# Softmax sums of two attention stages: from ones-matmuls on TensorE to column halving on GpSimd

## What is computed

```python
def _L1_xattn_ref(query, key, value, ...):      # causal; h = 16, hd = 8
    score = jnp.einsum('bqhd,bkhd->bhqk', q, k) / np.sqrt(hd)
    score = jnp.where(causal, score, -jnp.inf)
    probs = jax.nn.softmax(score, axis=-1)
    out = jnp.einsum('bhqk,bkhd->bqhd', probs, v).reshape(b, tq, d)
    return out @ Wo.T + bo
def _L2_xattn_ref(q, kv, Wq, Wkv, Wc):          # keys and values of one head's width, shared by 16 heads
    logits = jnp.einsum('bhld,bmd->bhlm', qh, mk) * scale
    attn = jax.nn.softmax(logits, axis=-1)
    out = jnp.einsum('bhlm,bmd->bhld', attn, mv)
```

## Time and profile before

| what | value |
|---|---|
| median of 3 runs | 3389.18 us (3385.43 to 3396.54) |
| profiled execution, its own time | 3393.09 us |
| span of the profiled execution | 3391.2 us |
| busy: PE / PEld / DVE / ACT / POOL | 79% / 54% / 65% / 36% / 13% of the span |
| layer 1 attention | about 410 to 735 us |
| layer 2 attention | about 1750 to 2135 us |

### The profile page before, as it was taken

The page is one execution under the profiler, slowest core; times in us unless marked ns, Lnnn a source line. Parts: engine busy times, 40 slices in busy tenths (PEclk is TensorE's granted clock), DMA queues, the critical chain, the costliest instruction groups (busy, mean ns, idle before and its releaser), DMA issues. The chain is left out here.

```text
span 3391.2 us, 66864 instructions
## 1 busy us (share of the span) xinstructions
PE 2683.7 (79%) x24521; PEld 1816.6 (54%) x24556; DVE 2218.8 (65%) x5515; ACT 1215.5 (36%) x1872; POOL 441.9 (13%) x749
## 2 busy tenths in 40 slices
PE   4867599958999999999978998797905658883456
PEld 4634356645666565666636666575704546662126
DVE  6889689963455555545437889772035558887668
ACT  3658688840000000000027776453301114442330
POOL 0022200000000000000000000241170004441003
PEclk9978699989999999999979999898957779997569
DMA  2010000012221212112100000101312210000001
GB/s 87 28 57 1 10 18 13 15 50 100 72 79 51 100 50 90 60 57 93 50 14 14 14 12 2 35 28 54 96 50 65 62 30 1 0 0 7 0 3 46
DMA packets 88410, 137.01 MB, mean 40 GB/s; under 512 B 42949, under 2 KB 54597, under 8 KB 87242
## 3 DMA queue, kind: packets, MB, share of 16 engines
q1 hardware_dynamic: 80746, 114.75, 10.5%
q0 software_dynamic: 7520, 20.34, 2.0%
HBM read 117.75 MB, written 17.30 MB: 40 GB/s over the span
## 5 line engine op out<-in xcount | busy, mean ns | idle before, releaser
L1435 PE MATMUL banks<-l1f_xe,l1f_w 128*128 128x512 f32 x1024 | 486.5, 598 | 10.4 <-DVE l1f_xe L1634 10.4
L1634 DVE TENSOR_TENSOR l1f_xe<-l1f_hT,l1f_rwb 128x512 f32<-128x512 f32 x256 | 173.5, 693 | 299.4 <-PE banks L1437 277.2
L1437 PEld LDWEIGHTS banks<-l1f_w,l1f_xe 128*128 128x128 f32 x2048 | 269.5, 192 | 122.9 <-issue 122.9
L1640 DVE TENSOR_TENSOR l1f_ae<-l1f_aoT,l1f_rwb 128x512 f32<-128x512 f32 x256 | 172.8, 691 | 160.2 <-PE banks L1465 155.8
L1437 PE MATMUL banks<-l1f_w,l1f_xe 128*128 128x128 f32 x2048 | 270.0, 275 | 0.0
L1435 PEld LDWEIGHTS banks<-l1f_xe,l1f_w 128*128 128x128 f32 x1024 | 177.3, 192 | 140.9 <-issue 126.9
L1465 PE MATMUL banks<-l1f_ae,l1f_w 128*128 128x512 f32 x512 | 225.2, 599 | 1.4 <-DVE l1f_ae L1640 1.4
L1465 PEld LDWEIGHTS banks<-l1f_ae,l1f_w 128*128 128x128 f32 x512 | 97.4, 193 | 117.9 <-issue 115.7
L223 PE MATMUL banks<-consts,l3p_h 128*128 128x128 f32 x64 | 17.8, 435 | 166.1 <-DVE l3p_h L140 166.1
L214 POOL COPY x<-xn 128x512 f32 (+1 forms) x16 | 9.8, 610 | 972.0 <-DVE xn L1664 972.0
L223 PEld LDWEIGHTS banks<-consts,l3p_h 128*128 128x128 f32 x64 | 11.5, 217 | 169.3 <-issue 132.2
(11 more groups left out here) (490 smaller groups left out, 6346.4 us busy)
## 6 DMA issues: line engine op xcount, KB each, us to landing
l1f_rwb<-l1f_shares SPq DMA_DIRECT2D x128, 512.0 KB, 4.3
l3p_ctx<-in_ctxT SPq DMA_DIRECT2D x32, 256.0 KB, 3.9
l0a_ctxT<-in_ctxT SPq DMA_DIRECT2D x16, 256.0 KB, 2.6
l2f_sent<-l0f_zero SPq DMA_DIRECT2D x4, 1024.0 KB, 7.0
l1a_ctxT<-in_ctxT SPq DMA_DIRECT2D x16, 256.0 KB, 2.6
l2c_ctxT<-in_ctxT SPq DMA_DIRECT2D x16, 256.0 KB, 2.6
l2e_rows<-l2f_sent SPq DMA_DIRECT2D x16, 256.0 KB, 2.8
l2f_answers<-l2e_y POOLq DMA_DIRECT2D x16, 256.0 KB, 2.7
```

Source lines behind the costliest of these rows:

```text
L1435: pe.matmul(bank, w[:, n, e, :], xe[:, e % NB, :], start=(e == 0), stop=(e == E - 1))
L1437: last = pe.matmul(v_bank[:, D * j:D * j + D], xe[:, e % NB, P * j:P * j + P], w[:, 2, e, :], start=(e == 0 and j == 0), stop=(e == E - 1) ...
L1634: dve.tensor_tensor(xe[:, e % NB, :], hT[:, m, :], rwb[:, m, e, :], ALU.mult).then_inc(s.xe_ready, 1)
L1640: dve.tensor_tensor(ae[:, e % NB, :], aoT[:, m, :], rwb[:, m, e, :], ALU.mult).then_inc(s.ae_ready, 1)
```

## The change

In both stages the sums no longer come from TensorE. A new part `total` on POOL adds the two halves of each head's 64 columns of `prob` (after the exponential): 64 to 32, 32 to 16, 16 to 8, three `tensor_tensor` adds of 128 x 512, 128 x 256 and 128 x 128 results, all in SBUF. `invert` on DVE sums the last 8 columns and takes the reciprocal of 16 numbers a token. `widen` on POOL copies each of the 16 numbers 8 times (128 x 128). `weigh` on PE transposes that one tile into PSUM in place of the eight ones-matmuls, and `normalise` on DVE copies it out of PSUM, where it took the reciprocal, before the same multiplication. `centre` has a further wait: for the first halving of two tiles before. In POOL's lists the new parts come between the old ones: layer 1 add_bias(n-1), widen(n-5), total(n-4), copy_mv(n-8); layer 2 keep_q(n-10), widen(n-15), total(n-14), copy_mv(n-19). On DVE `invert` stands behind `centre` and ahead of `normalise`.

```diff
     def weigh(self, pe, t, r):
+        pe.wait_ge(s.rec_ready, t + 1)
+        wait(pe, s.o_ready, t)
+        pe.transpose(self.rec_psum, self.rec[:, r % 2].rearrange("p h e -> p (h e)"), self.k.ident[:, :])
         pe.wait_ge(s.pT_ready, t + 1)
         pe.wait_ge(s.v_ready, t - j + TG)
-        wait(pe, s.o_ready, t)
-        for a in range(4):
-            for e in range(2):
-                pe.matmul(self.sum_psum[32 * a:32 * a + 32, :], self.k.pairsum[:, 32 * e:32 * e + 32], self.pT[:, r % 2, 2 * a + e, :],
-                          start=(e == 0), stop=(e == 1), skip_group_check=True)
...
         wait(dve, s.pT_psum, t - 1)
+        wait(dve, s.tree_chain, 2 * t - 3)
         dve.tensor_tensor(self.prob[:, r % 2], self.scores, self.top[:, :].unsqueeze(2).to_broadcast([P, H, S]),
                           ALU.subtract).then_inc(s.centred, 1)
+    def total(self, pool, t, r):
+        prob = self.prob[:, r % 2]
+        pool.wait_ge(s.exp_ready, t + 1)
+        settle(pool, self.k)
+        pool.tensor_tensor(self.half[:, :, :], prob[:, :, 0:S // 2], prob[:, :, S // 2:S], ALU.add).then_inc(s.tree_chain, 1)
+        pool.wait_ge(s.tree_chain, 2 * t + 1)
+        settle(pool, self.k)
+        pool.tensor_tensor(self.quarter[:, :, :], self.half[:, :, 0:S // 4], self.half[:, :, S // 4:S // 2], ALU.add).then_inc(s.tree_chain, 1)
+        pool.wait_ge(s.tree_chain, 2 * t + 2)
+        wait(pool, s.summed, t - 1)
+        settle(pool, self.k)
+        pool.tensor_tensor(self.eighth[:, r % 2], self.quarter[:, :, 0:S // 8], self.quarter[:, :, S // 8:S // 4], ALU.add)\
+            .then_inc(s.sum_ready, 1)
+    def invert(self, dve, t, r):
+        dve.wait_ge(s.sum_ready, t + 1)
+        settle(dve, self.k)
+        dve.tensor_reduce(self.sums[:, :], self.eighth[:, r % 2], AX_X, ALU.add).then_inc(s.summed, 1)
+        dve.wait_ge(s.summed, t + 1)
+        wait(dve, s.rec_ready, t)
+        dve.reciprocal(self.inverse[:, :], self.sums[:, :]).then_inc(s.inverted, 1)
+    def widen(self, pool, t, r):
+        pool.wait_ge(s.inverted, t + 1)
+        wait(pool, s.o_psum, t - 1)
+        settle(pool, self.k)
+        pool.tensor_copy(self.rec[:, r % 2], self.inverse[:, :].unsqueeze(2).to_broadcast([P, H, HD])).then_inc(s.rec_ready, 1)
     def normalise(self, dve, t, r):
         dve.wait_ge(s.o_psum, t + 1)
-        dve.reciprocal(self.rec[:, :], self.sum_psum).then_inc(s.rec_ready, 1)
-        dve.wait_ge(s.rec_ready, t + 1)
+        dve.tensor_copy(self.recT[:, :], self.rec_psum).then_inc(s.rec_copied, 1)
+        dve.wait_ge(s.rec_copied, t + 1)
         wait(dve, s.y_psum, t - 1)
-        dve.tensor_tensor(self.oT[:, r % 2], self.oT_psum, self.rec[:, :], ALU.mult).then_inc(s.o_ready, 1)
+        dve.tensor_tensor(self.oT[:, r % 2], self.oT_psum, self.recT[:, :], ALU.mult).then_inc(s.o_ready, 1)
```

More of the change, by code:

```diff
@@ L1004 @@
 CORE_SEMS = ("weights x_read biased xn_ready stats_chain stats_ready mv_copied q_ready k_ready v_ready score_psum max_ready "
-             "centred exp_ready pT_psum pT_ready o_psum rec_ready o_ready y_psum ")
+             "centred exp_ready tree_chain sum_ready summed inverted pT_psum pT_ready o_psum rec_ready rec_copied o_ready y_psum ")
 RING = 2 * TG
@@ L1023, in __init__ @@
         self.pT = sb("pT", [P, 2, 8, P])
-        self.rec = sb("rec", [P, P])
+        self.half = sb("half", [P, H, S // 2])
+        self.quarter = sb("quarter", [P, H, S // 4])
+        self.eighth = sb("eighth", [P, 2, H, S // 8])
+        self.sums = sb("sums", [P, H])
+        self.inverse = sb("inverse", [P, H])
+        self.rec = sb("rec", [P, 2, H, HD])
+        self.recT = sb("recT", [P, P])
         self.oT = sb("oT", [P, 2, P])
@@ L1029, in __init__ @@
         self.pT_banks = (ps[2], ps[3])
-        self.oT_psum, self.sum_psum = ps[4][:, 0:P], ps[4][:, P:2 * P]
+        self.oT_psum, self.rec_psum = ps[4][:, 0:P], ps[4][:, P:2 * P]
         self.y_psum = ps[5].rearrange("p (t c) -> p t c", c=D)
@@ L1107, in centre @@
         wait(dve, s.pT_psum, t - 1)
+        wait(dve, s.tree_chain, 2 * t - 3)
         dve.tensor_tensor(self.prob[:, r % 2], self.scores, self.top[:, :].unsqueeze(2).to_broadcast([P, H, S]),
                           ALU.subtract).then_inc(s.centred, 1)
+    def total(self, pool, t, r):
+        s = self.s
+        prob = self.prob[:, r % 2]
[11 more added lines that the diff above has]
+    def invert(self, dve, t, r):
+        s = self.s
+        dve.wait_ge(s.sum_ready, t + 1)
[5 more added lines that the diff above has]
+    def widen(self, pool, t, r):
+        s = self.s
+        pool.wait_ge(s.inverted, t + 1)
+        wait(pool, s.o_psum, t - 1)
+        settle(pool, self.k)
+        pool.tensor_copy(self.rec[:, r % 2], self.inverse[:, :].unsqueeze(2).to_broadcast([P, H, HD])).then_inc(s.rec_ready, 1)
     def normalise(self, dve, t, r):
@@ L1209, in _ @@
             pool.wait_ge(s.row_ready, 1)
-            pipeline(pool, k.NT, [(8, lambda t, r: core.copy_mv(pool, t, r)), (1, lambda t, r: core.add_bias(pool, t, r))],
+            pipeline(pool, k.NT, [(1, lambda t, r: core.add_bias(pool, t, r)), (5, lambda t, r: core.widen(pool, t, r)),
+                                  (4, lambda t, r: core.total(pool, t, r)),
+                                  (8, lambda t, r: core.copy_mv(pool, t, r))],
                      unroll=RING, behind=8)
@@ L1302, in feed @@
                     last.then_inc(s.x_read, TG)
-            pipeline(dve, k.NT, [(4, lambda t, r: core.centre(dve, t, r)), (6, lambda t, r: core.normalise(dve, t, r)),
+            pipeline(dve, k.NT, [(4, lambda t, r: core.centre(dve, t, r)), (5, lambda t, r: core.invert(dve, t, r)),
+                                 (6, lambda t, r: core.normalise(dve, t, r)),
                                  (7, lambda t, r: core.new_x(dve, t, r)), (0, feed)], unroll=RING, behind=8)
@@ L1743, in keep_q @@
                 pool.tensor_copy(core.qT[:, u, :], q[:, u, :]).then_inc(s.q_ready, TG)
-            pipeline(pool, k.NT, [(18, lambda t, r: core.copy_mv(pool, t, r)), (10, at_group(keep_q))], unroll=RING, behind=8)
+            pipeline(pool, k.NT, [(10, at_group(keep_q)), (15, lambda t, r: core.widen(pool, t, r)),
+                                  (14, lambda t, r: core.total(pool, t, r)),
+                                  (19, lambda t, r: core.copy_mv(pool, t, r))], unroll=RING, behind=8)
         @block.tensor
@@ L1888, in spread_v @@
                 last.then_inc(s.v_ready, TG)
-            pipeline(dve, k.NT, [(14, lambda t, r: core.centre(dve, t, r)), (16, lambda t, r: core.normalise(dve, t, r)),
+            pipeline(dve, k.NT, [(14, lambda t, r: core.centre(dve, t, r)), (15, lambda t, r: core.invert(dve, t, r)), (16, lambda t, r: core.normalise(dve, t, r)),
                                  (17, lambda t, r: core.add_x(dve, t, r)), (6, at_group(choose)), (8, at_group(store_v)),
```

## The result

The changed kernel takes 3431.78 us (median of 4 runs, 3422.11 to 3436.09) against 3390.76 for the kernel before beside it: a ratio of 1.0117, 95% interval [1.0088, 1.0145]. The interval lies above 1, so it is slower by more than the noise of the runs. The profiled execution took 3434.38 us with a span of 3432.8, 41.6 more than before.

The account below looks back on a forecast made before the run. It took DVE to limit two of four steps in layer 1, and PE two steps and DVE the `choose` step in layer 2. Layer 1 +25 us and layer 2 +5 us on 3389.2 gave 3419, range 3388 to 3452.

Parts of the forecast that it names:

- L1300 waits for POOL: Layer 1 layer norm on DVE: its SBUF instructions are held up by POOL's additions, 1.0 us a group.
- `choose` blocked: Layer 2, DVE: L1866 and the two comparisons L1873 wait for POOL's halvings, 1.0 us a group.
- `invert` waits 0.8 a group: Layer 1, DVE: POOL's sums come late for `invert`, by 0.3 and 0.5 us in two of four steps.
- step 2: Layer 1 step (tile modulo 4) with residual sum and statistics, limited by DVE; `invert` forecast 0.3 us late.
- step 0: Layer 1 step (tile modulo 4) with the layer norm, limited by DVE; `invert` forecast 0.5 us late.
- The earlier wait in `centre`: DVE's further wait for POOL's halving was to cost nothing, as it concerns work over 1 us back.
- I count no change of it: Granted clock, 0.98 in both stages before: taken to stay at the upper level, no time counted.
- The savings: Less work on DVE and PE: 0.25 us a group in layer 1, 2 x 0.29 plus 0.12 in layer 2.
- POOL as the bound: Rival: POOL's chain a tile takes over some 4.7 us and limits the group; +58 us, 3447; chance 0.13.
- nothing is blocked: Rival: sums late, but DVE slips through beside POOL; no change, 3391 us; chance 0.11.
- The adds are done in time: Rival: addition chain under 3.0 us, blocking under 0.2 a group, savings kept; -11 us, 3378; chance 0.08.
- The point on the reciprocal: Small SBUF reciprocal on DVE beside POOL's `add_bias`: up to 1.0 us a group if blocked; nothing counted.

Follow-up runs that it names:

- e1: Kernel before plus POOL's three additions, read by nobody, and the further wait in `centre`; sums still from PE: 3443.41 us, ratio 1.0171.
- e5: Changed kernel with layer norm ahead of `invert`, `add_bias` behind `total`, and every fourth tile's layer 2 halvings after the one-hot matrix: ratio 1.0019.
- e4: Changed kernel without the further wait in `centre`: ratio 1.0106 to the kernel before.
- e10: Changed kernel with the further wait in `centre` on another semaphore, `sum_ready` at t - 1 instead of `tree_chain` at 2 t - 3: ratio 1.0105.
- e6: Changed kernel with layer norm, `add_bias` and layer 2 halvings moved out of DVE's way, and without the further wait in `centre`: ratio 1.0005.
- e3: Changed kernel with eight more PE transposes a group, ahead of the h transposes (layer 1) and one-hot transposes (layer 2): ratio 1.0077.
- e2: Changed kernel with one 128 x 128 add for the three halvings (sums incomplete) and the further wait on `sum_ready`: ratio 0.9953.

## Why the prediction was right, and where it was not

The forecast of 3419 us, slower, with 3388 to 3452, was right in sign and held the time; it was 13 us short. Its main mechanism, POOL's long additions keeping DVE's instructions waiting, is shown. That the sum for layer 1 came so near is luck: too much for `invert` stands against two costs that were left out.

- **L1300 waits for POOL: right.** Forecast 1.0 us a group; measured 4 x (0.598 - 0.345) = 1.01. e1 and e5 show it as the cause: the stretch is there with additions that nobody reads, and gone when they are moved.
- **`choose` blocked: right.** Forecast 1.0; measured (1.096 - 0.425) + 2 x (0.550 - 0.419) = 0.93.
- **`invert` waits 0.8 a group: mis-sized.** In step 2 it starts 0.13 us after the subtraction's end (614.26 + 1.22 to 615.61), where it starts 0.07 before the end when nothing holds it (604.35 + 1.23 to 605.51): 0.2 late, forecast 0.3. In step 0 it is not late at 605.51; forecast 0.5. Over the groups of tiles 8 to 56 the means are 0.18 and 0.07 us, so 0.25 a group in place of 0.8. Three terms made the difference in step 0: from the end of the exponential to the last 8 columns it is 3.03 us and not 3.2, since POOL's hand-overs (ACT to POOL too) take 0.18 to 0.20 us and not 0.24; the distance from the subtraction before to this one, by which `invert` is due, was read from one group as 3.98 us where the mean before is 4.11; and it is 4.32 after, since the subtraction itself comes later now.
- **The earlier wait in `centre` "cost nothing": failed**, by 0.09 us a tile on the mean in layer 1 and 0.05 in layer 2 (e4, e10), some 6 us in all (e5 to e6). The argument looked at what is waited for, and not at what it costs to work out the value.
- **"I count no change of it", the clock: failed**, and is the largest miss: 1.3 us a group in layer 2, 21 us over 16 groups by the trace (e3), and up to 0.27 in layer 1. The blocking of `choose` was forecast, but not followed on to PE, which has its own savings to add to the same pause (that the savings lengthen it was not tested).
- **The savings: right.** Forecast 0.25 a group in layer 1 and 0.58 + 0.12 in layer 2; e2 has 0.33 and 0.69. With the copy at 0.235 us, DVE's part is 0.18 a tile, 0.36 over two steps.

So layer 2 was forecast at +0.3 and came to +1.50 a group; with the clock held up it is +0.18 (e3). Layer 1 was forecast at +1.55 and came to +1.48, with 0.55 us too much for `invert` against some 0.3 for the register work (0.26 from e5 to e6) and up to 0.27 for the clock left out. These two overlap, since the low turns fall in e4 and e10 as well, so the terms are not a sum to the last tenth.

Of the rivals, POOL as the bound fell with the shorter additions (0.742 and 0.453), "nothing is blocked" with L1338. "The adds are done in time" wanted a chain under 3.0 us, which came to 3.03, and blocking under 0.2 a group, which came to 1.0. The point on the reciprocal is settled: L1138 takes 253 to 254 ns in all 128 cases, 15 of which lie wholly inside a POOL addition. It did not wait. The Trainium skill, SBUF — State Buffer, section "Who interferes with whom", says that a DVE instruction with two SBUF inputs contends with a GpSimd instruction that reads SBUF, that copies and tensor_scalar can, and that one with at most one SBUF input otherwise does not. The trace agrees: L1907, the copies of `spread_v` and L1338 are held up, while L1135 (at most 289 ns) and the subtraction (at most 1226) are not, though 14 of the 128 reductions and 67 of the 128 subtractions overlap a POOL addition.

## What to carry to other kernels

Before work is moved to GpSimd, mark in the timeline which VectorE copies and tensor_scalars work from SBUF to SBUF and which instructions have two SBUF inputs, where they fall in the period, and whether a long GpSimd instruction will start in front of them; moving the two apart was worth about 1% here (1.0117 to 1.0019), and a better order of the rest made the change pay. A delay that is found on one engine has to be followed to the next: what VectorE lost in `choose` (0.93 us a group) cost more on TensorE, through its clock (1.3). And a wait that is long over is free only if its value is: here a counter that goes up by two a tile put a register instruction between two dependent instructions.

## What was not expected of the hardware

- In layer 2 a pause of PE of some 2 us was followed by a stretch at granted clock 0.50, in which eight transposes took 1.63 to 1.97 us instead of 1.09, in 11 of 16 groups; behind the pauses of 1.54 to 1.80 us in the kernel before they took 1.09. Extra transposes whose results nobody reads made the kernel some 0.4% faster (1.0117 to 1.0077, from two chips; 3422.74 in e4 to 3411.07 in e3 on one).
- One register instruction of 53 ns on DVE's sequencer, between two dependent instructions, made their distance 0.07 to 0.10 us longer in most of the tiles that have it; the semaphore wait that it serves costs nothing in the median (1.259 us in e10, 1.258 in e4).
